# Scanning in units of 64 steps with the carried state added by GpSimd, and a gate loop written out

## The reference, cut to what matters

```
x_proj = x @ W_in; xs, z = jnp.split(x_proj, 2, axis=-1)
delta = xs @ W_delta; Bv = xs @ W_B; Cv = xs @ W_C
deltaA = jnp.exp(jnp.einsum('bld,dn->bldn', delta, A))
deltaB = jnp.einsum('bld,bln->bldn', delta, Bv)
state = dA_i * state + dB_i * x_i[:, None, :]      # for each token i in turn
y = jnp.einsum('bdn,bn->bd', state, C_i)
y * jax.nn.silu(z) @ W_out, added to the tokens
```

## Time and profile before

| | |
|---|---|
| three runs | 6912.54, 6915.71, 6920.44 us; median 6915.71 |
| the profiled execution | 6921.82 us, of which the span from first to last instruction is 6920.0 |
| busy in the span | PE 6346.8 us (92%), DVE 6286.0 (91%), ACT 4605.5 (67%), POOL 2423.6 (35%) |
| mean granted TensorE clock | 0.975 of full speed |

### The profile page before, as it was taken

One profiled execution on the slowest core, in us unless ns is written; L12 is line 12 of the kernel. 1 busy time (PEld: TensorE's weight loads), 2 busy tenths in 40 slices (PEclk: granted clock), 3 DMA queues, 4 the chain that ended last, 5 costly groups with the idle time before them and its releaser, 6 DMA issues. The chain is left out here.

```text
span 6920.0 us, 147961 instructions
## 1 busy us (share of the span) xinstructions
PE 6346.8 (92%) x52737; PEld 4042.9 (58%) x52737; DVE 6286.0 (91%) x3976; ACT 4605.5 (67%) x9719; POOL 2423.6 (35%) x3276
## 2 busy tenths in 40 slices
PE   8999989999879999999999999999999999998867
PEld 4666735566546566565665666656666566665535
DVE  7888878888769999999999999999999999999962
ACT  7888868888546666666666666666666666666541
POOL 5555545555433233333333323333233332332200
PEclk9999999999979999999999999999999999999985
DMA  6666666666522122121121211212122121221164
GB/s 143 154 154 154 154 146 155 155 154 154 135 58 63 43 49 53 39 63 45 47 53 40 63 45 47 52 41 64 43 47 53 46 58 43 48 51 39 24 188 114
DMA packets 864186, 566.76 MB, mean 82 GB/s; under 512 B 594957, under 2 KB 768941, under 8 KB 863661
## 3 DMA queue, kind: packets, MB, share of 16 engines
q1 hardware_dynamic: 794045, 526.01, 32.0%
q0 software_dynamic: 69632, 34.22, 2.2%
HBM read 161.99 MB, written 125.17 MB: 41 GB/s over the span
## 5 line engine op out<-in xcount | busy, mean ns | idle before, releaser
L1057 DVE TENSOR_TENSOR_SCAN states<-decay,enter_ps 128x1024 f32<-128x1024 f32 x2048 | 4465.4, 2262 | 77.3 <-ACT enter_ps L905 74.5
L764 PEld LDWEIGHTS enter_ps<-s_steps,s_tokens 128*128 128x128 bf16 (+1 forms) x16384 | 1598.3, 129 | 1450.0 <-DVE states L1057 1217.2
L764 PE MATMUL enter_ps<-s_steps,s_tokens 128*128 128x128 bf16 (+1 forms) x16384 | 2116.4, 309 | 313.9 <-DVE states L1057 306.9
L890 ACT ACTIVATE decay<-rate_ps 128x504 f32<-128x504 f32 x4096 | 2196.5, 588 | 186.2 <-PE rate_ps L741 7.2
L741 PE MATMUL rate_ps<-s_wide,s_decays 128*128 128x256 bf16 x8192 | 1322.6, 283 | 15.4 <-ACT decay L890 7.7
L243 POOL TENSOR_TENSOR entered<-gates 128x512 f32<-128x512 f32 x512 | 900.4, 1759 | 889.0 <-ACT gates L203 889.0
L905 ACT COPY enter_ps<-states 128x16 f32<-128x16 f32 x1920 | 362.9, 189 | 1270.1 <-PE enter_ps L764 1267.4
L989 POOL DMA_DIRECT2D s_tokens<-tokens_dram x2176 | 1090.0, 509 | 153.5 <-PE enter_ps L764 115.2
L788 PE MATMUL y_ps<-states,spread 128*32 128x512 f32 x8320 | 1113.1, 607 | 0.8 <-ACT y_sb L913 0.8
L161 PE MATMUL pre<-rows,weights_left 128*32 128x512 f32 x8192 | 908.9, 596 | 36.3 <-POOL rows L236 23.8
L741 PEld LDWEIGHTS rate_ps<-s_wide,s_decays 128*128 128x128 bf16 x8192 | 890.7, 118 | 80.3 <-ACT decay L890 20.3
(11 more groups left out here) (145 smaller groups left out, 2456.5 us busy)
## 6 DMA issues: line engine op xcount, KB each, us to landing
rows<-feat SPq DMA_DIRECT2D x1024, 132.0 KB, 2.4
rows<-feat SPq DMA_DIRECT2D x512, 128.0 KB, 2.4
s_steps<-steps_dram SPq DMA_DIRECT2D x4096, 8.0 KB
rows<-feat SPq DMA_DIRECT2D x512, 127.8 KB, 2.4
s_wide<-rates_dram SPq DMA_DIRECT2D x1024, 32.0 KB, 1.9
s_tokens<-tokens_dram POOLq DMA_DIRECT2D x2048, 16.0 KB, 2.0
rates_dram<-parts SPq DMA_DIRECT2D x64, 384.0 KB, 3.3
steps_dram<-parts SPq DMA_DIRECT2D x64, 384.0 KB, 3.5
```

The source lines that it names most:

```text
L764: mm = pe.matmul(out.rearrange("p h l -> p l h"), tokens[s][0:n * TERMS, k, :], steps[s][0:n * TERMS, k, 0:n, d:d + half], start=True, sto ...
L890: act.activation(decay[i][:, HEADS // 2 * h:HEADS // 2 * (h + 1), 1:], rate_ps[h][:, :, 0:n], ACT.Exp).then_inc(decay_ready, 1)
L1057: dve.tensor_tensor_scan(out, factor, term, 0.0, ALU.mult, ALU.add).then_inc(scanned, 1)
```

## The change

Chunks hold 64 tokens, and there are 16 of them (`CPB`); the 17th, its tiles and its branches are gone. There is no leading column: token 0 of a chunk stands in column 0. For a chunk other than the first of an image, the state carried in is brought in like this:

- TensorE computes the entering terms of the first token of all 128 channels once more (`first_steps`, one product for chunk c+1 at g = 5 of chunk c), and ScalarE copies them to SBUF (`take_first_steps` at g = 7, into `at_first`).
- GpSimd in every unit (`carry`): the product of the first decay and the last state of the chunk before (16 columns), then a memset of that decay column to 0, then the sum with `at_first`.
- ScalarE's `carry` copies this sum over column 0 of `enter_ps`. In the first chunk of an image there is no carry, and the scan waits for `enter_ready` itself.

The exponentials run two units ahead of the scan and the `exponents` three ahead. GpSimd's other work is cut up and placed at units: the 8 token DMAs 3, 3, 2 at g = 1, 2, 3; the differences at g = 4, 5, 6 and, for the last of each stage, at g = 0 of the next chunk; `spread_out` at g = 5. `fill_inverse` goes from g = 5 to g = 4, the drain of the VARIANCE stage from g = 6 to g = 5, the inversion on VectorE from g = 4 to g = 3. In the gate stage `pipelined` writes out all images, y has 8 sheets of 128 tokens, and there are two `PIECES`.

```diff
 def pipelined(eng, *pieces):
     depth = max(behind for behind, _ in pieces)
-    lead = (depth + 1) // 2 * 2
...
+    for n in range(BATCH + depth):
         for behind, piece in pieces:
             if 0 <= n - behind < BATCH:
                 piece(n - behind, (n - behind) % 2, (n - behind) // 2)
-    with eng.Fori(lead // 2, BATCH // 2) as turn:
...
-CPB = CROWD + 1
+CPB = LEN // SPAN
...
+            def first_steps(b, c):
+                s = set_of(c)
+                pe.wait_ge(enter_in[s], SCAN0 + (turn_of(b, c) + 1) * BLOCK * DMA)
+                pe.wait_ge(tokens_in[s], (turn_of(b, c) + 1) * TERMS * DMA)
+                pe.wait_ge(drained, stages_to(b + 1, c) if b + 1 < BATCH else stages_to(b + 1, 0))
+                pe.wait_ge(at_first_ready, firsts_to(b, c))
+                pe.matmul(work_ps[:, 0:INNER], tokens[s][:, 0, :], steps[s][:, 0, 0, :], start=True, stop=True
+                          ).then_inc(first_filled, 1)
...
-                if not ending or u + 2 < UPB:
-                    exponents(*following(b, u + 2))
+                if not ending or u + 3 < UPB:
+                    exponents(*following(b, u + 3))
...
+                if g == 5 and c + 1 < CPB:
+                    first_steps(b, c + 1)
...
             def carry(b, c, g, i):
-                act.wait_ge(enter_ready, units_to(b, c) + g + 1)
...
+                if c:
+                    act.wait_ge(enter_ready, units_to(b, c) + g + 1)
+                    act.wait_ge(added, carries_to(b, c) + g + 1)
+                    act.wait_ge(decay_reset, carries_to(b, c) + g + 1)
+                    act.copy(enter_ps[i][:, :, 0], at_first[set_of(c)][:, HEADS * g:HEADS * g + HEADS]).then_inc(carried, 1)
...
+                act.copy(at_first[set_of(c)][:, :], work_ps[:, 0:INNER]).then_inc(at_first_ready, 1)
...
-                if not ending or u + 1 < UPB:
-                    decays_of(*following(b, u + 1))
+                if not ending or u + 2 < UPB:
+                    decays_of(*following(b, u + 2))
+                if g == 7 and c + 1 < CPB:
+                    take_first_steps(b, c + 1)
...
+            def carry(b, c, g):
+                if c:
+                    n, i, mine = carries_to(b, c) + g, g % 2, slice(HEADS * g, HEADS * g + HEADS)
+                    pool.wait_ge(decay_ready, halves_to(b, c) + 2 * g + 2)
+                    pool.wait_ge(scanned, units_to(b, c - 1) + g + 1)
+                    pool.wait_ge(added, n - 1)
+                    pool.sem_inc(passed, 1)
+                    pool.tensor_tensor(product[i][:, :], decay[g % RING][:, :, 0], states[set_of(c - 1)][:, mine, SPAN - 1],
+                                       ALU.mult).then_inc(product_ready, 1)
+                    pool.wait_ge(product_ready, n + 1)
+                    pool.memset(decay[g % RING][:, :, 0], 0.0).then_inc(decay_reset, 1)
+                    pool.wait_ge(at_first_ready, firsts_to(b, c) + 1)
+                    pool.tensor_tensor(at_first[set_of(c)][:, mine], at_first[set_of(c)][:, mine], product[i][:, :], ALU.add
+                                       ).then_inc(added, 1)
...
+                for u in range(UPB):
+                    c, g = u // GROUPS, u % GROUPS
+                    carry(b, c, g)
+                    if g in (1, 2, 3) and not (ending and c + 1 == CPB):
+                        load_tokens(*((b, c + 1) if c + 1 < CPB else (b + 1, 0)), range(3 * g - 3, min(3 * g, TERMS)))
+                    if g == 5:
+                        spread_out(b, c)
+                    if not ending:
+                        if g == 0 and c:
+                            differences(b + 1, c - 1, LATE)
+                        differences(b + 1, c, g)
...
-    TOKENS = 2 * FULL
-    PIECES = ((0, 4, TOKENS), (4, 4, TOKENS), (8, 1, LAST))
+    TOKENS = 2 * SPAN
+    PIECES = ((0, 4, TOKENS), (4, 4, TOKENS))
```

More of the change, by code:

```diff
@@ L736, in exponents @@
                     pe.wait_ge(rates_in[s], SCAN0 + (turn_of(b, c) + 1) * QUAD * DMA)
[L737 to L748, removed]
+                for h in range(2):
+                    pe.wait_ge(decay_ready, halves_to(b, c) + g * 2 + h - 1)
+                    for q in range(2):
+                        mm = pe.matmul(rate_ps[h][:, QUAD * q:QUAD * q + QUAD, :], decays[:, g, 2 * h + q, :],
                                        wide[s][:, g, :, :], start=True, stop=True)
@@ L757, in enters @@
                 pe.wait_ge(scanned, units_to(b, c) + g - 1)
[L758 to L765, removed]
-                else:
-                    out = enter_ps[i][:, :, :].rearrange("p h l -> p (h l)")[:, 0:HEADS * (LAST + 1)]
-                    out = out.rearrange("p (h l) -> p h l", h=HEADS)[:, :, 1:]
-                    mm = pe.matmul(out.rearrange("p h l -> p l h"), tokens[s][:, 0, :],
-                                   steps[s][:, 0, :, HEADS * g:HEADS * g + HEADS], start=True, stop=True)
@@ L771, in enters @@
-                mm.then_inc(enter_ready, 1)
+                for k in range(BLOCKS):
+                    for h in range(2):
+                        d, half = HEADS * g + HEADS // 2 * h, HEADS // 2
+                        out = enter_ps[i][:, half * h:half * h + half, BLOCK * k:BLOCK * k + BLOCK]
+                        mm = pe.matmul(out.rearrange("p h l -> p l h"), tokens[s][:, k, :],
+                                       steps[s][:, k, :, d:d + half], start=True, stop=True)
+                mm.then_inc(enter_ready, 1)
@@ L823, in _ @@
                     unit(b, u, b == 0, b == BATCH - 1)
-            for g in range(2, GROUPS):
-                contract(BATCH - 1, CROWD - 1, g)
-            contract(BATCH - 1, CROWD, 0)
+            for g in range(GROUPS):
+                contract(BATCH - 1, CPB - 1, g)
         @block.scalar
@@ L937, in _ @@
                     unit(b, u, b == 0, b == BATCH - 1)
-            for q in (SHEETS - 2, SHEETS - 1):
-                move_y(BATCH - 1, q)
+            move_y(BATCH - 1, SHEETS - 1)
         @block.gpsimd
@@ L1014, in _ @@
             for n in range(len(STAGES)):
-                differences(0, n)
-            load_tokens(0, 0)
-            spread_out(0, 0)
+                for slot in range(LATE + 1):
+                    differences(0, n, slot)
+            load_tokens(0, 0, range(TERMS))
             for b in range(BATCH):
```

251 lines of the change are left out of this document (101 added, 150 removed).

## The result

The changed kernel takes 6799.0 us (median of 4 runs, 6798.22 to 6802.18) where the kernel before took 6917.34 (4 runs beside it): ratio 0.983, 95% interval 0.9813 to 0.9847. The forecast was 6793, with a range of 6768 to 6880. The profiled execution took 6799.73 us, its span 6797.9, so 122.1 us less than before; the forecast span was 6797.0.

The account below looks back on a forecast made before the run. VectorE's back-to-back scans were taken as the bound. Profiled 6921.8 us, less 120 and 14, plus 9, 0 and 2, is 6798.8; with the median 6.1 under the profiled execution, 6793 us, range 6768 to 6880.

Parts of the forecast that it names:

- Part 1: Scans on VectorE: chunk 17's short scans and waits go, 7.51 us in each of 16 images, gain 120 us.
- Part 2: TensorE: the added `first_steps` product, 0.13 us a chunk, is hidden in idle time; cost 0.
- Part 3: ScalarE: the added copy at g = 7 delays the next carry copy at c = 4, 8, 10; 9 us.
- Part 4: GpSimd's new product, memset and sum fit beside its DMAs and subtractions; cost 0.
- C: Length of GpSimd's product, memset and sum in a unit: taken as 0.75 us, no stall up to 0.9.
- Part 5: Start of an image and VARIANCE chunk: 0.1 us an image lost, 2 us in all.
- Part 6: Gate loop written out: the square root's table load moves ahead of its wait, 11 steps from 9.08 to 7.8, gain 14 us.
- the third piece: Gate stage: dropping it saves 0.1 us a step, which lies within the limit set by loads, so nothing is gained.
- The floor of 7.8: Gate stage: the load of z and x1, 7.6 us in all, keeps a step from going much under 7.8 us.
- The strides: GpSimd's strided operands: product near 0.2 us by the trace; a cacheline penalty of unknown size could make it dearer.
- the long chain: Rival: GpSimd's three dependent instructions take 1.45 us or more, giving 6938 us or far more, slower; chance 0.10.
- The rivals of the chain: GpSimd's three instructions take 1.0 to 1.3 us, 25 to 105 lost, chance 0.20; or 1.45 or more, 145 lost, 0.10.

Follow-up runs that it names:

- e3: The changed kernel with an exponential in place of the VARIANCE stage's square root, so no second table is loaded there: 6796.16 us, ratio 0.9824.
- e9: e2 with the inverse's 16 products cut into two halves, the drain and `first_steps` at g = 6: 6780.98 us, ratio 0.9796.
- e1: The kernel before with only the gate stage's loop written out: 6904.11 us, ratio 0.998.
- e8: The changed kernel with the exponentials one unit ahead of the scan and the exponents two, as in the kernel before: 6853.99 us.
- e2: The changed kernel with the 8 token DMAs of a chunk issued by SyncE instead of GpSimd: 6782.2 us, ratio 0.9801.
- e7: The changed kernel with all 8 token DMAs of a chunk at g = 1 instead of 3, 3, 2 at g = 1, 2, 3: 7019.98 us.

## Why the prediction was right, point by point

The time came 6 us over the forecast, and the span within 0.9, but that closeness is in part luck: losses and gains that were both priced too small cancelled. The 6 us are the 6.1 that I took off because the profiled execution before lay that far over its median; the one after lies 0.7 over its own.

- **Part 1, 120 us.** Right. With the long scans unchanged, the scans' stretch of before without chunk 17 is 4594.6 - 120.2 = 4474.4; after it is 4499.2, and the 24.8 between are nearly the waits of 25.5.
- **Part 2, 0.** `first_steps` itself cost nothing that shows. What I didn't look at is `fill_inverse`, moved ahead of it: 1.09 us of TensorE in one piece, which made the wait of 0.43 (e3, and e9 with its reservation).
- **Part 3, 9 us at g = 7 of c = 4, 8, 10.** Wrong, it was 0. No wait stands there: all 45 are accounted for elsewhere. The trace shows why. ScalarE's copies of the carry on both sides of such a unit (c = 4), and the scan that the second one feeds:

```profile
2903.99 0.17 ACT L859 COPY enter_ps<-at_first 128x16 f32<-128x16 f32 x1 [0.58 <-PE enter_ps L727]
...
2906.40 0.19 ACT L859 COPY enter_ps<-at_first 128x16 f32<-128x16 f32 x1
...
2907.12 2.26 DVE L1039 TENSOR_TENSOR_SCAN states<-decay,enter_ps 128x1024 f32<-128x1024 f32 x1
```

  The unit takes ScalarE 2.41 us and not 2.9, since instructions that follow one another without a wait overlap a little there, where I had added them up with gaps between. The copy ends 0.53 us ahead of its scan, no later than in a plain place (0.54 at g = 0 of chunk 10).
- **Part 4, C = 0.75 and no cost.** C is 0.60, and the single prices were near: 0.24, 0.125 and 0.22 where I had 0.2, 0.12 and 0.2. (The row of 1.26 that I called a product, for the bound from above, is a subtraction; the product took 1.04.) The sum "GpSimd has room" was right for the work that I counted. The step that failed is the one that took the 8 DMAs at 4.0 us, by a row of before: it leaves out the 0.23 ahead of each group, though the earlier trace rows has 0.30 ahead of the 8, and the pause of 3.14 once in 120 DMAs, which no row of before shows. Cost 16 us, which the forecast had at 0.
- **Part 5, 2 us.** The VARIANCE chunk cost 9.3 us; of its two waits the smaller is the table loads (e3), the larger the inverse.
- **Part 6, 14 us.** The mechanism was right and the 11 steps gave 15.4 (13.8 by the writing out alone, e1). The whole stage gave 24.1: I left out the entry of the loop (4.0) and priced the third piece at nothing (5.8, at the start 3.7 of it). The floor of 7.8 was 7.69, and TensorE waits there for the loads, as I had it. As for the drain of 1380 ns that the Trainium skill, page "ScalarE: Activation LUTs", section "What ACT_TABLE_LOAD costs", adds: the square root starts at 6527.60, when the load begun at 6526.26 has just ended at 6527.54, so the trace does not agree.
- **The strides.** GpSimd's product of 16 strided elements takes 0.243, its sum of dense ones 0.220. What the penalty could do here was 0.02 us, far from the long chain. (My remark that no page of the Trainium skill gives its size for GpSimd was wrong; here the measurement decides.) The scans kept their 2261 ns beside GpSimd's new reads; the Trainium skill, page "GPSIMD Engine Reference", section "1. Specifications", names contention with VectorE only for instructions of VectorE with two SBUF inputs (or a two-port mode), and a scan here has one input in SBUF and one in PSUM. The trace agrees.

In sum: expected waits of 11 us were 25.5, which is 14 more; the gate gave 10 us more than forecast and the start 2.3, which I had at nothing. The rivals of the chain were priced too low: C = 1.24 costs 233 us and is slower than before, where I had 25 to 105 us for C of 1.0 to 1.3 and the turning point at 1.45. As the true C was half of 1.24, it changed nothing in the time, but the chances that I gave to "slower" rested on a wrong threshold.

## What to carry to other kernels

Before small dependent work is put on an engine that also issues DMAs, lay out its queue with the gaps and pauses around those DMAs, and ask what is the longest piece that can stand ahead of the critical one; here the same chain cost 233 us or nothing, depending on who issued the loads. A wait in a row of scans that overlap costs its length and also the lost overlap, here 0.11 us each time. And where a number comes out right, check its terms singly: here errors of 14 us one way and 12 the other cancelled.

## What the runs showed of the hardware that was not expected

- GpSimd stands still for 3.14 us once in about 120 DMAs that it issues (2.95 at DMAs of half the size), ahead of the first of a group, in every run here that has these DMAs in groups between other work (the changed kernel, e3 to e8), besides 0.23 ahead of each group and 0.50 for each DMA whatever its bytes.
- SyncE is no quicker at issuing: 8 of the same token DMAs took it 5.01 us in e2 (next row), GpSimd 4.03 in e7. The gain of e2 is that the 15 waits behind GpSimd's pause are gone. The Trainium skill, page "DMA: Bandwidth & Descriptors", section "Issuing engine by pattern", calls the path of Sync and ScalarE generally faster; for the issue itself the trace does not agree.

```profile
3120.15 5.01 SPq L613 DMA_DIRECT2D s_tokens<-tokens_dram  x8
```

- The table load of ScalarE stands ahead of the wait where the code is written out and behind it in the loop (rows above and the earlier trace rows). Written out, an image of the gate stage took 1.25 us less (e1), nearly the load's 1.28.
